# Combine weights of the routed rounds: spread to all partitions by a DMA instead of a one-hot matrix product and a copy from PSUM

## The chip, the cores and the metric

One core of a Trainium2 chip runs the whole program. The metric is the device time of one execution in microseconds (us), median of the runs shown. TensorE (PE) multiplies, VectorE (DVE), ScalarE (ACT) and GpSimd (POOL) work elementwise, SyncE (SP) issues DMAs. Each engine takes its own instructions in order, and they wait for one another on semaphores.

## The reference

The program is a chain of eight blocks on 4 x 256 tokens of 128 features: four attention blocks and four feed-forward blocks, each added to x. The change touches the second block only, four rounds of a mixture of four experts with two chosen for each token:

```python
def more_forward(x, Wg, bg, W1, b1, W2, b2):     # x: layer norm of the stream, 1024 tokens x 128
    cur = x
    for r in range(4):
        flat = cur.reshape(-1, h)
        logits = flat @ Wg[r] + bg[r]
        vals, idx = jax.lax.top_k(logits, 2)
        w = jax.nn.softmax(vals, axis=-1)
        cw = jnp.sum(jax.nn.one_hot(idx, 4) * w[..., None], axis=1)      # 1024 x 4, zero for the experts not chosen
        hmid = jax.nn.gelu(jnp.einsum('nh,ehf->enf', flat, W1) + b1[:, None, :])   # 512 hidden features
        y = jnp.einsum('enf,efh->enh', hmid, W2) + b2[:, None, :]
        cur = cur + jnp.einsum('ne,enh->nh', cw, y).reshape(b, s, h)
    return cur
```

All experts are computed for all tokens, and the combine weight cw of an expert scales its output for each token.

## The kernel before

`routed_rounds` (line 1270) computes this with features on the partitions and tokens along the free dimension. The 1024 tokens are two halves of 512. A **turn** s is one round of one half (8 turns, the halves in alternation), and an **item** g = 4s + e is one expert e in one turn (32 items). What an item does:

- TensorE, `up(g)` (L1349): 12 products of 128x128 by 128x512, four feature tiles times three passes of a high and low split of the operands. `down(g)` (L1359): 12 more, into one PSUM bank.
- ScalarE, `hidden(g)` (L1434): the gelu of the four tiles out of PSUM, and a copy of half of them as high part (L1439). GpSimd copies the other half (L1590).
- VectorE, `split_hidden(g)` (L1504): the low parts. `combine(g)` (L1539, L1541): (down + b2) times the combine weight, then added to the running tokens curT.

Once in a turn there is the routing: `route(s)` (L1370) for the logits, some 18 tiny VectorE operations (`choose_first`, `choose_second`, `weigh_two`, the last at L1524), a tanh on ScalarE (L1462), `turn_weights(s)` (L1377), which transposes the weights to 4 rows (experts) x 512 tokens in PSUM bank 6, and `take_weights(s)` (L1458), ScalarE's copy of these rows into the tile cwT (partitions 0 to 3).

`combine` needs the row of its expert on all 128 partitions, since features are on partitions and the weight belongs to the token. Before the change `split_weights(s)` (VectorE, L1529) adds a low part of the four rows at partitions 32 to 35. `spread_weights(g)` (TensorE, L1389) multiplies a one-hot matrix `choose` of 36x128 by cwT (36x512) into bank 7, which puts row e on all partitions, and `take_spread(g)` (ScalarE, L1445) copies bank 7 to the tile spread[e]. There are four spread tiles, one for each expert. Two zeroings on ScalarE and two GpSimd operations (L1582) build `choose` and the rows of zeros once, before the first turn.

The order is written out by hand. In loop step g TensorE issues up(g), then the turn's transposes if a turn begins (e is 0), spread_weights(g-1), the routing product of the next turn if e is 1, and down(g-1). VectorE issues the routing operations due in this step, split_hidden(g), split_weights(s) if a turn begins, and combine(g-1). ScalarE issues hidden(g), take_weights(s) if a turn begins, and take_spread(g-1). SyncE has nothing in this stage before the change. Its next DMAs (L652, four loads for the following block) stand right behind the block before.

Of the kernel before, what the change touches and what calls it, by code (L numbers as in the profile page):

```python
# [23 lines left out]
P = 128  # L24
# [1245 lines left out]
def routed_rounds(k, name, number, E, W, ahead):  # L1270
# [11 lines left out]
    TURNS = 2 * ROUNDS  # L1282
    ITEMS = TURNS * E
    TPH = NT // 2
    LOW = 32
    shape = [P, TPH, E]
    hidden_part = [[k.parts[i][:, b * FT * HALF:(b + 1) * FT * HALF].rearrange("p (f n) -> p f n", f=FT) for b in range(2)]
                   for i in range(2)]
    cur_part = [k.parts[i][:, 2 * FT * HALF:2 * FT * HALF + T] for i in range(2)]
    cwT, choose = k.parts[2][:, 0:T], k.parts[2][:, T:T + E * P]  # L1290
    rows_of_parts = (slice(0, E), slice(LOW, LOW + E))
    w1_part = [k.split[i][:, 0:E * HALF].rearrange("p (e f) -> p e f", e=E) for i in range(2)]
    w2_part = [k.split[i][:, E * HALF:2 * E * HALF].rearrange("p (e f d) -> p e f d", e=E, f=FT) for i in range(2)]
    k.carve_from(0)
    H = [k.carve(F32, FT, HALF) for _ in range(2)]
    spread = [k.carve(F32, HALF) for _ in range(E)]
    logits, tagged, sel1, sel2, low, cw = (k.carve(F32, TPH, E) for _ in range(6))
    m1, m2, top, th, w1, w2 = (k.carve(F32, TPH) for _ in range(6))
    weighted = k.xn[:, :, :].rearrange("p t d -> p (t d)")
# [8 lines left out]
    tanh_ready = count("tanh_ready", TURNS)  # L1308
    cw_ready = count("cw_ready", TURNS)
    cwT_psum = count("cwT_psum", TURNS)  # L1310
    cwT_high = count("cwT_sb", TURNS)
    cwT_low = count("b2_psum", TURNS)
    spread_psum = k.count("rounds_spread_psum", ITEMS)
    cur_high = count("turned", TURNS)
    cur_low = count("T_ready", TURNS)
    up_psum = count("up_psum", FT * ITEMS)
    h_ready = count("h_ready", FT * ITEMS)
    down_psum = count("down_psum", ITEMS)
    combined = count("combined", ITEMS)
    chooser = k.count("rounds_chooser", 2)  # L1320
    rows_psum = k.count("rounds_rows_psum", 2)
    spread_sb = k.count("rounds_spread_sb", ITEMS)
    zeros = k.count("rounds_zeros", 2)
    high_pool = k.count("rounds_h_high", ITEMS)
    k.slots_filled = k.count("packed_fill_done", 4)
    FILL_AT = 8
# [11 lines left out]
    def tensor(pe):  # L1338
        bank = k.bank

        def up(g):
            s, e = g // E, g % E
            if e == 0:
                pe.wait_ge(*cur_low.at(s + 1))
            for f in range(FT):
                if g >= 1:
                    pe.wait_ge(*h_ready.at(FT * (g - 1) + f + 1))
                for n, (a, b) in enumerate(PASSES):
                    ins = pe.matmul(bank[f], w1_part[a][:, e, f * P:(f + 1) * P], cur_part[b][:, half_of(s % 2)],  # L1349
                                    start=n == 0, stop=n == len(PASSES) - 1)  # L1350
                ins.then_inc(up_psum.semaphore, 1)

        def down(g):
            if g >= 2:
                pe.wait_ge(*combined.at(g - 1))
            for f in range(FT):
                pe.wait_ge(*h_low.at(2 * g + f // 2 + 1))
                for n, (a, b) in enumerate(PASSES):
                    ins = pe.matmul(bank[4 + g % 2], w2_part[a][:, g % E, f, :], hidden_part[b][g % 2][:, f, :],  # L1359
                                    start=f == 0 and n == 0, stop=f == FT - 1 and n == len(PASSES) - 1)  # L1360
            ins.then_inc(down_psum.semaphore, 1)

        def route(s):
            if s >= 2:
                pe.wait_ge(*combined.at(E * (s - 1)))
            if s >= 1:
                pe.wait_ge(*cwT_low.at(s))
            for t in range(TPH):
                at = (s % 2) * HALF + t * P
                ins = pe.matmul(bank[6][:, t * E:(t + 1) * E], curT[:, at:at + P], W("router")[:, s // 2, :],  # L1370
                                start=True, stop=True)
            ins.then_inc(logits_psum.semaphore, 1)

        def turn_weights(s):
            pe.wait_ge(*cw_ready.at(s + 1))
            for t in range(TPH):
                ins = pe.transpose(bank[6][0:E, t * P:(t + 1) * P], cw[:, t, :], k.ident[:, :])  # L1377
            ins.then_inc(cwT_psum.semaphore, 1)

        def spread_weights(g):  # L1380

            s, e = g // E, g % E
            if e == 0:
                pe.wait_ge(*cwT_low.at(s + 1))
                if s == 0:
                    pe.wait_ge(*chooser.at(2))
            if g >= 1:
                pe.wait_ge(*spread_sb.at(g))
            pe.matmul(bank[7], choose[0:LOW + E, e * P:(e + 1) * P], cwT[0:LOW + E, half_of(s % 2)],  # L1389
                      start=True, stop=True).then_inc(spread_psum.semaphore, 1)  # L1390

        def rows_of(h, dst):
            pe.wait_ge(*combined.at(ITEMS - E * (1 - h)))
            for t in range(TPH):
                at = h * HALF + t * P
                ins = pe.transpose(dst[:, t * P:(t + 1) * P], curT[:, at:at + P], k.ident[:, :])
            ins.then_inc(rows_psum.semaphore, 1)

        k.norm.tensor(pe, use, k.xn)
        pe.wait_ge(k.norm.T_ready, 2 * use + 2)  # L1400
        pe.wait_ge(k.weights[name], 16)
        route(0)
        pe.wait_ge(ahead.parts_ready, 1)
        for g in range(ITEMS + 1):
            s, e = g // E, g % E
            if g < ITEMS:
                up(g)
            if g == 1:
                turn_weights(0)
            elif e == 0 and 0 < s < TURNS:  # L1410
                turn_weights(s)
            if g > 1:
                spread_weights(g - 1)
            if e == 1 and 0 < s + 1 < TURNS:
                route(s + 1)
            if g >= 1:
                down(g - 1)
            if g == 1:
                spread_weights(0)
            if g == ITEMS - 1:  # L1420
                rows_of(0, bank[6])
        rows_of(1, bank[0])

    def scalar(act):
# [13 lines left out]
            act.wait_ge(*h_ready.at(FT * (g + 1)))  # L1438
            act.activation(two(hidden_part[0][g % 2], 1), two(H[g % 2], 1), ACT.Copy).then_inc(high_act.semaphore, 1)  # L1439

        def take_spread(g):
            act.wait_ge(*spread_psum.at(g + 1))
            if g >= E:
                act.wait_ge(*combined.at(g - E + 1))
            act.activation(spread[g % E], bank[7], ACT.Copy).then_inc(spread_sb.semaphore, 1)  # L1445

        def split_current(s):
            if s >= 2:
                act.wait_ge(*combined.at(E * (s - 1)))
# [3 lines left out]

        def take_weights(s):
            act.wait_ge(*cwT_psum.at(s + 1))
            if s == 0:
                act.wait_ge(*chooser.at(2))
            act.activation(cwT[0:E, half_of(s % 2)], bank[6][0:E, :], ACT.Copy).then_inc(cwT_high.semaphore, 1)  # L1458

        def weigh(s):  # L1460
            act.wait_ge(*margin.at(s + 1))
            act.activation(th, m2, ACT.Tanh, scale=0.5).then_inc(tanh_ready.semaphore, 1)  # L1462

        act.wait_ge(k.x_tiles, NT * number)
        for part, words in ((cwT[0:LOW, :], T), (choose[0:LOW + E, :], E * P)):
            n = part.shape[0]
            act.activation(part.rearrange("p (a n) -> p a n", n=P), k.ident[0:n, :].unsqueeze(1).broadcast_to([n, words // P, P]),
                           ACT.Copy, scale=0.0).then_inc(zeros.semaphore, 1)
        k.norm.scalar(act, use, curT)
        split_current(0)  # L1470
        split_current(1)
        for g in range(ITEMS + 1):
# [10 lines left out]
                take_weights(s)  # L1483
            if e == 1 and 2 <= s + 1 < TURNS:
                split_current(s + 1)
            if g >= 1:
                take_spread(g - 1)

    def vector(dve, chain):
        bank = k.bank  # L1490
# [32 lines left out]
            chain.then(dve.tensor_tensor(sel2, sel2, w2.unsqueeze(2).broadcast_to(shape), ALU.mult))  # L1523
            dve.tensor_tensor(cw, sel1, sel2, ALU.add).then_inc(cw_ready.semaphore, 1)  # L1524

        def split_weights(s):
            dve.wait_ge(*cwT_high.at(s + 1))
            cols = half_of(s % 2)
            dve.tensor_tensor(cwT[LOW:LOW + E, cols], bank[6][0:E, :], cwT[0:E, cols].bitcast(F32), ALU.subtract)\  # L1529
                .then_inc(cwT_low.semaphore, 1)  # L1530

        def combine(g):
            s, e = g // E, g % E
            dve.wait_ge(*down_psum.at(g + 1))
            dve.wait_ge(*spread_sb.at(g + 1))
            if g >= 2:
                dve.wait_ge(*combined.at(g))
            mine, cols = weighted[:, half_of(g % 2)], half_of(s % 2)
# [14 lines left out]
        for g in range(ITEMS + 1):  # L1553
# [10 lines left out]
                choose_second(s + 1)  # L1564
            if g < ITEMS:
                split_hidden(g)
            if g == 1:
                split_weights(0)
            elif e == 0 and 0 < s < TURNS:
                split_weights(s)  # L1570
            if g >= 1:
                combine(g - 1)
        add_rows(0, bank[6])
# [2 lines left out]

    def gpsimd(pool):
        k.norm.gpsimd(pool, use)
        pool.wait_ge(*zeros.at(2))
        for part in rows_of_parts:  # L1580
            rows = choose[part, :].rearrange("p (e n) -> p e n", e=E)
            pool.affine_select(out=rows, in_=rows.bitcast(F32), compare_op=ALU.not_equal, fill=1.0, base=0,  # L1582
                               pattern=[[-1, E], [0, P]], channel_multiplier=1).then_inc(chooser.semaphore, 1)
            n = rows_of_parts.index(part) + 1
            pool.wait_ge(*chooser.at(n))
        for g in range(ITEMS):
            if g >= 2:
                pool.wait_ge(*down_psum.at(g - 1))
# [5 lines left out]
                    .then_inc(k.slots_filled.semaphore, 1)  # L1594

    def sync(sp):
        pass

    return tensor, scalar, vector, gpsimd, sync

# [1443 lines left out]
class Kit:  # L3044
# [92 lines left out]
    def open_rounds(self):  # L3137

        self.work_extent.close()
        self.work_extent.enter_context(self.nc.sbuf_tensor("kept_for_l1x", [P, REGION_B], F32))  # L3140
        parts = 2 * PARTS + T + HALF
        flat = self.work_extent.enter_context(self.nc.sbuf_tensor("parts", [P, parts], F32R))
        self.parts = [flat[:, 0:PARTS], flat[:, PARTS:2 * PARTS], flat[:, 2 * PARTS:]]
        self.work = self.work_extent.enter_context(self.nc.sbuf_tensor("rounds_work", [P, WORK - REGION_B - parts], F32))

    def open_later(self):
# [266 lines left out]
```

## Time and profile before

| | us |
|---|---|
| runs | 1202.22, 1204.62, 1211.36 |
| median | 1204.62 |
| span of the profiled execution | 1202.7 |

| engine | busy us | share of the span |
|---|---|---|
| TensorE | 1047.4 | 87% |
| VectorE | 811.3 | 67% |
| ScalarE | 665.8 | 55% |
| GpSimd | 387.2 | 32% |

These shares are means over eight blocks. The routed rounds are the stretch from about 124 to 347 us of the span. Busy times of an engine are sums of its instructions. "issue" as the releaser of a wait means that the engine waited for nothing that the profile shows. PEld is TensorE's load of the stationary operand, which can run beside a product. In a view of DMAs the stretch asked for is cut into 40 equal slices, and each value is the rate of one slice in GB/s, or the mean busy share of the core's 16 DMA engines in tenths.

### The profile page before, as it was taken

To read this page: it belongs to the slowest core of one execution; us is meant where nothing else is said; L and a number is where in the kernel's file an instruction comes from. 1 tells how busy PE (TensorE), PEld (TensorE's weight loads), DVE (VectorE), ACT (ScalarE), POOL (GpSimd) and SP (SyncE) were. 2 spreads that over 40 slices of the span, in tenths; PEclk is the share of its full clock that TensorE was granted. 3 is DMA by queue.
4 is the path that set the end of the run, shared out by engine and by line. 5 is a ranking of instruction groups with operands and counts; after the bars stand their busy time and mean duration, and the time that the engine had idled before them with its cause. 6 is when DMAs were issued, how large, how long until landed. Compare 5 with 4: busy or idle time off the path is not lost.

```text
span 1202.7 us, 18102 instructions
## 1 busy us (share of the span) xinstructions
PE 1047.4 (87%) x5942; PEld 735.0 (61%) x5942; DVE 811.3 (67%) x1977; ACT 665.8 (55%) x1640; POOL 387.2 (32%) x608
## 2 busy tenths in 40 slices
PE   3587899999976989878899999998699899999677
PEld 2345677777741333655667677776568566668565
DVE  5763588887866867258788777667755566665563
ACT  3253566666642757456677877777134466665121
POOL 5220112111111101034655657557300344443200
PEclk8687799999985989989899999999599999999779
DMA  6503000000004330030000000030600100000000
GB/s 217 111 10 104 1 1 6 9 1 1 1 26 145 132 91 3 1 140 1 1 1 1 1 1 1 1 140 1 251 1 2 72 2 1 2 1 2 1 1 18
DMA packets 26572, 45.08 MB, mean 37 GB/s; under 512 B 3536, under 2 KB 23792, under 8 KB 25200
## 3 DMA queue, kind: packets, MB, share of 16 engines
q1 hardware_dynamic: 23936, 41.57, 10.2%
q10 hardware_dynamic: 2544, 2.36, 0.6%
q8 instruction: 48, 0.79, 0.3%
q14 instruction: 44, 0.36, 0.1%
HBM read 36.94 MB, written 6.82 MB: 36 GB/s over the span
## 4 chain that ended last, share of the span: by engine, by line
PE 41%; ACT 9%; DVE 8%; issue 3%; POOL 2%; DMA 1%; DVEq 0%; SPq 0%; ACTq 0%; POOLq 0%
PE psum L1736 7%; ACT region_d L1802 4%; PE psum L2397 3%; PE psum L2450 3%; PE psum L2381 2%; ACT region_c L1819 2%; PE psum L2364 2%; PE psum L1773 2%; PE psum L1750 2%; PE psum L2359 2%; PE psum L2807 1%; PE psum L409 1%; PE psum L2356 1%; PE psum L2404 1%; PE psum L1053 1%
## 5 line engine op out<-in xcount | busy, mean ns | idle before, releaser
L1736 PE MATMUL psum<-gated_parts 128*128 128x512 f32 x768 | 198.8, 412 | 15.0 <-DVE region_d L1906 10.9
L1736 PEld LDWEIGHTS psum<-gated_parts 128*128 128x128 f32 x768 | 141.3, 192 | 68.3 <-DVE region_d L1906 30.9
L1987 POOL TENSOR_TENSOR region_d<-region_d 128x256 f32<-128x256 f32 x126 | 99.5, 790 | 114.4 <-DVE region_d L1906 114.0
L1434 ACT ACTIVATE rounds_work<-psum,region_c 128x512 f32<-128x512 f32 x128 | 87.0, 689 | 59.3 <-PE psum L1349 59.3
L787 DVE TENSOR_REDUCE work<-psum 128x1 f32<-128x512 f32 x128 | 81.8, 685 | 28.0 <-PE psum L365 26.4
L1359 PE MATMUL psum<-parts,split 128*128 128x512 f32 x384 | 97.6, 404 | 0.0
L1802 ACT ACTIVATE region_d<-psum,gated_work 128x128 f32<-128x128 f32 x256 | 75.8, 451 | 36.8 <-issue 26.2
L1349 PE MATMUL psum<-parts,split 128*128 128x512 f32 x384 | 94.4, 396 | 0.0
L1590 POOL CAST parts<-rounds_work 128x1024 fp32r<-128x1024 f32 x32 | 33.4, 1044 | 179.7 <-ACT rounds_work L1434 179.7
L1504 DVE TENSOR_TENSOR parts<-rounds_work,parts 128x1024 fp32r<-128x1024 f32 x64 | 77.5, 1223 | 20.3 <-POOL parts L1590 17.4
L1906 DVE SCALAR_TENSOR_TENSOR region_d<-psum,gated_work,region_d 128x128 f32<-128x128 f32 x256 | 71.4, 344 | 29.0 <-ACT region_d L1802 20.6
L1906 DVE SCALAR_TENSOR_TENSOR region_d<-psum,ctx,region_d 128x128 f32<-128x128 f32 x256 | 71.4, 343 | 24.1 <-ACT region_d L1802 21.0
L2475 ACT ACTIVATE null_work<-psum,null_work 128x257 f32<-128x257 f32 x128 | 59.7, 472 | 47.9 <-DVE null_work L2533 47.9
L1802 ACT ACTIVATE region_d<-psum,ctx 128x128 f32<-128x128 f32 x256 | 73.5, 383 | 20.5 <-PE psum L1736 16.3
L1349 PEld LDWEIGHTS psum<-parts,split 128*128 128x128 f32 x384 | 73.5, 192 | 15.7 <-issue 0.2
L1359 PEld LDWEIGHTS psum<-parts,split 128*128 128x128 f32 x384 | 70.9, 191 | 19.6 <-issue 6.1
L545 ACT ACTIVATE work<-psum 128x1024 f32<-128x1024 f32 x64 | 65.1, 1024 | 26.6 <-PE psum L379 24.2
L133 POOL TENSOR_TENSOR rstd<-var_eps,minus_half 128x4 f32<-128x4 f32 x12 | 12.3, 1023 | 186.8 <-DVE var_eps L93 186.7
L2533 DVE TENSOR_REDUCE null_work<-psum 128x2 f32<-128x514 f32 x64 | 43.9, 688 | 38.4 <-PE psum L2381 38.4
L2621 POOL TENSOR_TENSOR null_work<-null_work 128x512 f32<-128x512 f32 x64 | 66.6, 1040 | 0.0
L365 PE MATMUL psum<-work 48*128 48x512 bf16 x128 | 53.0, 450 | 13.7 <-DMA work<-q_parts 10.5
L2546 DVE COPY null_work<-psum 128x512 f32<-128x512 f32 x64 | 43.3, 678 | 4.0 <-PE psum L2397 3.6
(433 smaller groups left out, 2189.4 us busy)
## 6 DMA issues: line engine op xcount, KB each, us to landing
region_a<-in_l1v SPq DMA_DIRECT2D x1, 4096.0 KB, 14.4
region_b_last<-in_l1o SPq DMA_DIRECT2D x1, 4096.0 KB, 12.4
region_a<-in_l2f SPq DMA_DIRECT2D x1, 4096.0 KB, 13.5
region_b_last<-in_l3f_small SPq DMA_DIRECT2D x1, 4096.0 KB, 19.8
region_a<-in_l3f SPq DMA_DIRECT2D x1, 2080.0 KB, 7.3
region_c<-in_l0f SPq DMA_DIRECT2D x1, 2076.0 KB, 12.2
region_c<-in_l3x SPq DMA_DIRECT2D x1, 2048.0 KB, 7.9
ctx_parts<-front_work SPq DMA_DIRECT2D x6, 256.0 KB, 3.8
```

Of the source, the lines that this page charges most:

```text
L545: act.activation(PT[s % 2].rearrange("p (a n) -> p a n", a=2), k.pair(2 + 2 * (s % 2)), ACT.Exp, scale=scale).then_inc(p2_exp.semaphore, 1)
L787: dve.tensor_reduce(NM[:, b, heads[0]:heads[0] + HPG, t], bank[g % 2][:, :].rearrange("p (j n) -> p j n", j=HPG), AX.X, ALU.max, negate=Tr ...
L1349: ins = pe.matmul(bank[f], w1_part[a][:, e, f * P:(f + 1) * P], cur_part[b][:, half_of(s % 2)], start=n == 0, stop=n == len(PASSES) - 1)
L1359: ins = pe.matmul(bank[4 + g % 2], w2_part[a][:, g % E, f, :], hidden_part[b][g % 2][:, f, :], start=f == 0 and n == 0, stop=f == FT - 1 a ...
L1434: act.activation(H[g % 2][:, f, :], bank[f], ACT.Gelu_apprx_tanh, bias=W("b1")[:, (g % E) * FT + f:(g % E) * FT + f + 1]).then_inc(h_ready ...
L1504: dve.tensor_tensor(two(hidden_part[1][g % 2], c), two(H[g % 2], c), two(hidden_part[0][g % 2], c).bitcast(F32), ALU.subtract).then_inc(h_ ...
L1736: ins = pe.matmul(bank[2 * (n % 2) + c], src[a][:, t * P:(t + 1) * P], weights[b][:, piece(c)], start=m == 0, stop=m == len(PASSES) - 1)
L1802: ins = act.activation(scaled[n % RING][:, e, :], bank[2 * (n % 2)][:, e * P:(e + 1) * P], ACT.Copy, scale=scalars[:, n % NT, e:e + 1])
L1906: ins = dve.scalar_tensor_tensor(out=tile, in0=bank[2 * (n % 2) + 1][:, e * P:(e + 1) * P], scalar=scalars[:, n % NT, HALF_E + e:HALF_E + ...
L1987: pool.tensor_tensor(tile[:, 0:2, :], tile[:, 0:2, :], tile[:, 2:4, :], ALU.add).then_inc(k.pool_chain, 1)
L2475: ins = act.activation(PR[g % 4][:, t, :], bank[2 * (g % 2) + t][:, 0:NK], ACT.Exp, bias=NM[:, g % 4, t:t + 1], accum_out=den[:, g % 4, t: ...
L2621: pool.tensor_tensor(PR[g % 4][:, :, 0:S], PR[g % 4][:, :, 0:S], r.broadcast_to([P, TPB, S]), ALU.mult)\
```

## The change

For each turn, SyncE waits until the four rows are in cwT and issues one DMA for each expert, which reads that expert's row of 512 fp32 values (2 KB, one partition) 128 times and writes spread[e] on all 128 partitions (256 KB). From the second turn on, each DMA also waits until the last turn's combine of the same expert has read spread[e]. The one-hot product, its ScalarE copy, the low part of the rows, the one-hot matrix and its set-up go. cwT is now plain fp32.

```diff
-        def spread_weights(g):
-            s, e = g // E, g % E
-            if e == 0:
-                pe.wait_ge(*cwT_low.at(s + 1))
...
-            pe.matmul(bank[7], choose[0:LOW + E, e * P:(e + 1) * P], cwT[0:LOW + E, half_of(s % 2)],
-                      start=True, stop=True).then_inc(spread_psum.semaphore, 1)
...
-        def take_spread(g):
-            act.wait_ge(*spread_psum.at(g + 1))
-            if g >= E:
-                act.wait_ge(*combined.at(g - E + 1))
-            act.activation(spread[g % E], bank[7], ACT.Copy).then_inc(spread_sb.semaphore, 1)
...
-        def split_weights(s):
-            dve.wait_ge(*cwT_high.at(s + 1))
-            cols = half_of(s % 2)
-            dve.tensor_tensor(cwT[LOW:LOW + E, cols], bank[6][0:E, :], cwT[0:E, cols].bitcast(F32), ALU.subtract)\
-                .then_inc(cwT_low.semaphore, 1)
...
             if s >= 1:
-                pe.wait_ge(*cwT_low.at(s))
+                pe.wait_ge(*cwT_sb.at(s))
...
             dve.wait_ge(*down_psum.at(g + 1))
-            dve.wait_ge(*spread_sb.at(g + 1))
+            dve.wait_ge(*spread_loaded[e].at(16 * (s + 1)))
...
     def sync(sp):
-        pass
+        for s in range(TURNS):
+            sp.wait_ge(*cwT_sb.at(s + 1))
+            for e in range(E):
+                if s >= 1:
+                    sp.wait_ge(*combined.at(E * (s - 1) + e + 1))
+                sp.dma_start(spread[e], cwT[e:e + 1, half_of(s % 2)].unsqueeze(1).broadcast_to([1, P, HALF])).then_inc(spread_loaded[e].semaphore, 16)
```

SyncE, between the weight loads that end the first block (in_l2f_small) and the loads for the third (ctx_parts), the change against before:

```order
+L1549 DMA rounds_work<-rounds_work 128x1x512 [waits experts_cwT_sb]
+L1549 DMA rounds_work<-rounds_work 128x1x512 x3
+L1549 DMA rounds_work<-rounds_work 128x1x512 [waits experts_combined,experts_cwT_sb]
+L1549 DMA rounds_work<-rounds_work 128x1x512 [waits experts_combined] x3
 L652 DMA work<-ctx_parts 48x4x256 [waits c_stored,packed_fill_done]
 L652 DMA work<-ctx_parts 48x4x256
```

The pair of rows of the second turn comes seven times, for turns 1 to 7: 32 DMAs stand ahead of the four loads L652, which were next in line before.

TensorE at the start of turn 2, before (L1377 are the transposes, L1389 the one-hot product, L1359 down, L1349 up):

```order
L1377 MATMUL psum<-ident,rounds_work 4x128 [waits experts_cw_ready]
L1377 MATMUL psum<-ident,rounds_work 4x128 x3
L1389 MATMUL psum<-parts 128x512 [waits rounds_spread_sb]
L1359 MATMUL psum<-parts,split 128x512 [waits rounds_h_low,experts_combined]
L1359 MATMUL psum<-parts,split 128x512 x2
```

and with the change (L1371 are the transposes, L1353 is down):

```order
L1371 MATMUL psum<-ident,rounds_work 4x128 [waits experts_cw_ready]
L1371 MATMUL psum<-ident,rounds_work 4x128 x3
L1353 MATMUL psum<-parts,split 128x512 [waits rounds_h_low,experts_combined]
L1353 MATMUL psum<-parts,split 128x512 x2
L1353 MATMUL psum<-parts,split 128x512 [waits rounds_h_low]
```

The one-hot product is gone from between up and down, and nothing takes its place on this engine.

VectorE at the start of a turn, before:

```order
L1504 TENSOR_TENSOR parts<-rounds_work,parts 128x1024 [waits rounds_h_high]
L1504 TENSOR_TENSOR parts<-rounds_work,parts 128x1024 [waits rounds_high_act]
L1529 TENSOR_TENSOR parts<-psum,parts 4x512 [waits experts_cwT_sb]
L1539 SCALAR_TENSOR_TENSOR xn<-psum,region_c,rounds_work 128x512 [waits experts_combined,rounds_spread_sb,experts_down_psum]
L1541 TENSOR_TENSOR xnT<-xnT,xn 128x512 [waits vector_chain]
```

and with the change (L1467 are the low parts of the hidden tiles, L1496 and L1498 the combine of the last item of the turn before):

```order
L1467 TENSOR_TENSOR parts<-rounds_work,parts 128x1024 [waits rounds_h_high]
L1467 TENSOR_TENSOR parts<-rounds_work,parts 128x1024 [waits rounds_high_act]
L1496 SCALAR_TENSOR_TENSOR xn<-psum,region_c,rounds_work 128x512 [waits experts_combined,rounds_spread3,experts_down_psum]
L1498 TENSOR_TENSOR xnT<-xnT,xn 128x512 [waits vector_chain]
L1467 TENSOR_TENSOR parts<-rounds_work,parts 128x1024 [waits rounds_h_high]
L1467 TENSOR_TENSOR parts<-rounds_work,parts 128x1024 [waits rounds_high_act]
```

The split of the weights is gone, and each combine waits for the DMA of its expert (`rounds_spread3`), with the low parts of the next item queued behind it.

## Rows read from the trace of the kernel before

**Rows 1.** The page's first line: the profiled execution.
```profile
span 1202.7 us, 18102 instructions
```

**Rows 2.** Busy time by stretch: routed rounds, then one turn of them.
```profile
core 0: us, PE busy (x) PEld busy (x) DVE busy (x) ACT busy (x) POOL busy (x), PEclk, DMA share, GB/s
140.00:345.00 205.00, 200.65 (x857) 151.81 (x857) 159.33 (x261) 136.50 (x202) 34.92 (x34) 0.99 0.01 3
188.50:214.55 26.05, 25.43 (x113) 19.41 (x112) 21.07 (x37) 17.76 (x28) 6.84 (x7) 1.00 0.06 16
```

**Rows 3.** Who waited for whom, 140 to 345 us: total, times, longest us.
```profile
PEld psum L1389 <- issue: 10.2, 32, 0.4
PE psum L1377 <- DVE rounds_work L1524: 4.4, 7, 0.6
```

**Rows 4.** Timeline of TensorE across items: start us, us, engine, line, xcount [idle before].
```profile
204.45 2.88 PE L1349 MATMUL psum<-parts,split 128*128 128x512 f32 x12
207.26 0.50 PE L1389 MATMUL psum<-parts 36*128 36x512 f32 x1
207.69 2.99 PE L1359 MATMUL psum<-parts,split 128*128 128x512 f32 x12
210.52 2.88 PE L1349 MATMUL psum<-parts,split 128*128 128x512 f32 x12
```

**Rows 5.** Timeline, all engines, where a turn begins.
```profile
210.72 0.75 DVE L1539 SCALAR_TENSOR_TENSOR xn<-psum,region_c,rounds_work 128x512 f32<-128x512 f32 x1 [0.24 <-PE psum L1359]
211.50 0.69 DVE L1541 TENSOR_TENSOR xnT<-xnT,xn 128x512 f32<-128x512 f32 x1
...
212.93 1.03 DVE L1524 TENSOR_TENSOR rounds_work<-rounds_work 128x16 f32<-128x16 f32 x1
...
214.02 0.60 PE L1377 MATMUL psum<-ident,rounds_work 128*4 128x128 f32 x4 [0.62 <-DVE rounds_work L1524]
...
215.18 0.57 ACT L1458 ACTIVATE parts<-psum 4x512 fp32r<-4x512 f32 x1
...
216.56 0.68 DVE L1529 TENSOR_TENSOR parts<-psum,parts 4x512 fp32r<-4x512 f32 x1
```

**Rows 6.** Timeline where the first turn's weights are ready.
```profile
136.29 0.59 ACT L1458 ACTIVATE parts<-psum 4x512 fp32r<-4x512 f32 x1 [0.20 <-PE psum L1377]
137.90 0.68 DVE L1529 TENSOR_TENSOR parts<-psum,parts 4x512 fp32r<-4x512 f32 x1
...
140.36 4.62 PE L1359 MATMUL psum<-parts,split 128*128 128x512 f32 x12
```

**Rows 7.** Timeline at the stage's end: the last combine.
```profile
346.57 0.69 DVE L1541 TENSOR_TENSOR xnT<-xnT,xn 128x512 f32<-128x512 f32 x1
```

**Rows 8.** DMA issues of the page: mask_bias; then two stretches' GB/s, 15.8:16.4 and 17.6:18.2.
```profile
front_work<-mask_bias SPq DMA_DIRECT2D x4, 4.0 KB
...
GB/s 0 0 0 0 0 0 0 0 0 0 0 0 0 0 0 0 0 0 0 0 0 0 0 0 0 0 0 0 0 68 0 69 0 34 34 0 35 34 0 0
...
GB/s 0 0 0 0 0 0 0 0 0 0 0 0 0 0 0 0 0 0 0 0 0 0 0 34 34 68 1 34 1 34 34 0 34 0 0 0 0 0 0 0
```

**Rows 9.** DMA share and GB/s, 38:42; then one window, 100 to 101 us.
```profile
DMA  9999999989999999999999999999999999999999
GB/s 251 246 256 215 200 190 200 184 149 215 220 246 287 266 174 159 179 189 149 118 118 159 133 118 118 133 154 169 179 174 169 154 154 226 236 241 195 215 277 246
...
front_work<-q_parts SPq DMA_DIRECT2D x3, 64.0 KB
...
100.00:101.00 1.00, 1.00 (x9) 0.75 (x11) 0.00 (x0) 0.98 (x1) 0.00 (x0) 0.50 1.02 428
```

**Rows 10.** SyncE's timeline in the stage; then GB/s by slice, 208:214.
```profile
208.79 1.79 SPq L652 DMA_DIRECT2D work<-ctx_parts  x4
...
GB/s 0 0 0 0 0 0 0 0 0 0 0 34 150 208 191 188 171 219 205 171 212 181 150 137 242 157 7 0 0 0 0 0 0 0 0 0 0 0 0 0
```

More of the change, by code:

```diff
@@ L1284, in routed_rounds @@
     TPH = NT // 2
-    LOW = 32
     shape = [P, TPH, E]
@@ L1289, in routed_rounds @@
     cur_part = [k.parts[i][:, 2 * FT * HALF:2 * FT * HALF + T] for i in range(2)]
-    cwT, choose = k.parts[2][:, 0:T], k.parts[2][:, T:T + E * P]
-    rows_of_parts = (slice(0, E), slice(LOW, LOW + E))
     w1_part = [k.split[i][:, 0:E * HALF].rearrange("p (e f) -> p e f", e=E) for i in range(2)]
@@ L1296, in routed_rounds @@
     spread = [k.carve(F32, HALF) for _ in range(E)]
+    cwT = k.carve(F32, T)
     logits, tagged, sel1, sel2, low, cw = (k.carve(F32, TPH, E) for _ in range(6))
@@ L1310, in routed_rounds @@
     cwT_psum = count("cwT_psum", TURNS)
-    cwT_high = count("cwT_sb", TURNS)
-    cwT_low = count("b2_psum", TURNS)
-    spread_psum = k.count("rounds_spread_psum", ITEMS)
+    cwT_sb = count("cwT_sb", TURNS)
+    spread_loaded = [k.count(f"rounds_spread{e}", 16 * TURNS) for e in range(E)]
     cur_high = count("turned", TURNS)
@@ L1411, in tensor @@
                 turn_weights(s)
-            if g > 1:
-                spread_weights(g - 1)
             if e == 1 and 0 < s + 1 < TURNS:
@@ L1417, in tensor @@
                 down(g - 1)
-            if g == 1:
-                spread_weights(0)
             if g == ITEMS - 1:
@@ L1455, in take_weights @@
             act.wait_ge(*cwT_psum.at(s + 1))
-            if s == 0:
-                act.wait_ge(*chooser.at(2))
-            act.activation(cwT[0:E, half_of(s % 2)], bank[6][0:E, :], ACT.Copy).then_inc(cwT_high.semaphore, 1)
+            act.activation(cwT[0:E, half_of(s % 2)], bank[6][0:E, :], ACT.Copy).then_inc(cwT_sb.semaphore, 1)
         def weigh(s):
@@ L1462, in weigh @@
             act.activation(th, m2, ACT.Tanh, scale=0.5).then_inc(tanh_ready.semaphore, 1)
[L1464 to L1468, printed above, removed]
         k.norm.scalar(act, use, curT)
@@ L1485, in scalar @@
                 split_current(s + 1)
-            if g >= 1:
-                take_spread(g - 1)
     def vector(dve, chain):
@@ L1566, in vector @@
                 split_hidden(g)
[L1567 to L1570, printed above, removed]
             if g >= 1:
@@ L1578, in gpsimd @@
         k.norm.gpsimd(pool, use)
[L1579 to L1585, printed above, removed]
         for g in range(ITEMS):
@@ L3140, in open_rounds @@
         self.work_extent.enter_context(self.nc.sbuf_tensor("kept_for_l1x", [P, REGION_B], F32))
-        parts = 2 * PARTS + T + HALF
+        parts = 2 * PARTS
         flat = self.work_extent.enter_context(self.nc.sbuf_tensor("parts", [P, parts], F32R))
-        self.parts = [flat[:, 0:PARTS], flat[:, PARTS:2 * PARTS], flat[:, 2 * PARTS:]]
+        self.parts = [flat[:, 0:PARTS], flat[:, PARTS:2 * PARTS]]
         self.work = self.work_extent.enter_context(self.nc.sbuf_tensor("rounds_work", [P, WORK - REGION_B - parts], F32))
```

7 lines of the change are left out of this document (removed).

## The prediction

> **What bounds the kernel now.** I read the busy times by stretch first. In the routed rounds TensorE is busy 200.65 of 205 us at a granted clock of 0.99, VectorE 159.33, and the DMA engines 0.01 of the time [rows 2]. So TensorE sets this stage, and the DMA side is free. A turn of four items is 26.05 us, with VectorE busy 21.07 of it, so VectorE is the next bound, five us behind. The waits say the same: TensorE's idle time in the stage is some 0.32 us ahead of each of the 32 one-hot products (10.2 us in all, "issue") and 4.4 us ahead of the transposes L1377, for VectorE [rows 3]. The timeline gives the item: up starts at 204.45 and the next up at 210.52, which is 6.07 us, 0.43 of it from the one-hot product to down (207.26 to 207.69) [rows 4].
>
> **What the change takes away.** On TensorE, 32 products of 0.43 us, and up to 0.32 us of idle time ahead of each: 13.8 to 24 us of the engine that sets the stage. On ScalarE (17.76 us busy in a turn) and VectorE it takes a copy in each item and L1529 in each turn (0.68 us [rows 5]). ScalarE is hidden behind TensorE today, so that is worth nothing by itself. The first routing product after the start no longer waits for L1529 but for ScalarE's copy, 138.58 against 136.88 [rows 6], which is 1.7 us. The set-up of the one-hot matrix stood beside the layer norm and is costed at nothing. What hides it is TensorE's wait for the norm, and it is gone in any case.
>
> **What the change adds.** 32 DMAs of 256 KB. Each reads one row of one partition 128 times. Combine(g) waits for its DMA. Behind combine(g-1) on VectorE stand the routing operations of the next step and the low parts of item g+1. TensorE's down(g+1) waits for these, and so, in the end, does everything.
>
> What one such DMA costs is the question. 256 KB over all partitions would be short: the load between 100 and 101 us moved 428 GB/s with the 16 engines full [rows 9], so 0.6 us plus latency. The trace has two kinds of transfer that don't reach this. The loads of 38 to 42 us, 64 KB ones among them, go to few partitions (16 to 48). There the engines are as busy (share 9 tenths and more in nearly every slice), but the rate falls to 118 GB/s [rows 9]. Full engines and a quarter of the rate mean that the packets wait for something on the side of the few partitions. The nearest relative of the new DMA is mask_bias: 4 KB in 8 packets of 512 B, all from a row on one partition, as here [rows 8]. Each slice is 15 ns, so 34 GB/s in a slice is one packet. The first packets start in the 30th slice and the last in the 38th, 120 ns for seven steps. In the other stretch it is the 24th to the 33rd slice, 135 ns. That is 17.1 and 19.3 ns for 512 B, 26 to 30 GB/s, though eight packets could be on eight engines at once. For 2 KB it is 69 to 77 ns, and for 128 of them 8.8 to 9.9 us. With an uncertainty of a slice each way (105 to 150 ns) it is 7.7 to 11.0 us. I take 9.6 us, between the mean of the two stretches (9.3) and the slower of them, since the first packets find the source idle and these seven steps are short for a steady rate.
>
> The Trainium skill has a rule for this (SBUF — State Buffer, "Door 1: The DMA port swizzle"): DMA bandwidth goes with the number of ports that the partitions reach, 27.2 GB/s each, and partitions 0 to 3 share one port. Rows 8 and the fall in rows 9 agree with it. By it the four rows of cwT have one port together, a DMA is 262144 B / 27.2 GB/s = 9.64 us as an estimate, and the stage would come out 1.3 us later than by my price.
>
> **Does the stream stay full?** If the transfers of one turn follow one another, a turn of DMAs is 4 x 9.6 = 38.4 us against TensorE's 26.05. At a turn's start there could be a gap, because the next rows wait for routing. From the start of a combine (210.72) to the end of ScalarE's copy of the rows (215.75) it is 5.03 us [rows 5]. From issue to the first bytes it is 0.86 us (208.79 to the 12th slice of 0.15 us, 209.65 [rows 10]). Together 5.9 us. This chain starts when the third DMA of a turn has landed, and the fourth then runs for another 9.6 us. So the next turn's first DMA is in the queue 3.7 us before the fourth ends: no gap. The wait for the old spread tile is behind by a whole turn for experts 0 to 2, and for expert 3 it ends 1.5 us after the fourth landed, when three others are queued.
>
> TensorE will now wait, and its clock may fall. At the lower level of its clock 12 products took 4.62 us [rows 6], so an item takes 9.24 us. That is still under 9.6, and routing adds a little. So even then the DMAs set the pace. The price of a low clock is 0 to 5 us in all, and I take 0. The loads L652 go from 208.79 us to behind all 32. They have 384 KB in all and took some 2.4 us [rows 10]. They land right behind the last spread, before the next block has made its own operands, so they cost nothing. If that cover is missing, it is those 2.4 us.
>
> **The sum.** The first rows are ready at 136.88 [rows 6]. First bytes 0.86 later: 137.7. 32 x 9.6 = 307.2, so the last byte at 444.9. About 1 us until the wait ends (no row shows it, 0 to 2), and 1.5 us for combine (0.75 + 0.69 with gaps, rows 5): 447.4. Before, the last combine ends at 347.26 [rows 7]. The stage ends 100.1 us later, the rest is unchanged, and TensorE's 14 to 24 us are lost behind the wait. 1202.7 [rows 1] + 100.1 = 1302.8. The median of the runs is 1.9 above this execution: **1304.7**, so 1305 us. With 7.7 and 11.0 us for a DMA it is 1244 and 1350.
>
> **Rivals.** (A) The above, slower by 100 us: 82%.
>
> (B) Reading one row many times is no limit, and a DMA lands within some 3 us of its issue. For it: in rows 8 the engines' queues may just have been fed at this pace. The skill's fit (DMA: Bandwidth & Descriptors, "Anatomy of one DMA"; about 2.0 us plus bytes at 436 GB/s, measured for GpSimd's queue) would give 2.6 us as an estimate. Against it: two kinds of transfer, the fewer partitions the slower. Then the DMA is hidden: the rows are ready at 215.75, and the turn's first combine comes an item and a half later. TensorE gives back 0.43 + 0.32 us in 32 items, 24 us, and 1.7 at the start. VectorE's chain ahead of L1377 doesn't get shorter, so that wait grows by up to 0.75 us in seven turns, 5 us back. 1204.6 - 21 = about 1184. The point from which it decides is a price below 5.3 us an item (6.07 - 0.75), 50 GB/s from one partition. 12%.
>
> (C) Something between: 5.5 to 7 us. Equality is where 32 items take as long as now: (347.26 - 2.5 - 137.7) / 32 = 6.5 us. Turns would then show gaps of 5.9 us less the price. 1185 to 1220, 3%.
>
> (D) Many engines on one row hinder each other more than in rows 8, over 11 us: above 1350, 3%. The floor, 118 GB/s over 16 partitions, would give 7.4 GB/s and 35 us, but rows 8 exclude this.
>
> (E) The DMA doesn't use 16 engines but few or one. That changes little in time if one engine moves about 27 GB/s (428 / 16 in rows 9), 9.8 us for 256 KB. It is a variant of A by its time, within its chance, and told apart by the DMA share: near one sixteenth here, near full in A.
>
> **How the numbers follow.** A is the likeliest and gives the time. 1265 to 1350 us is 8.4 to 11.0 us for a DMA and holds nearly all of A, about 8 in 10. About 1% is what a measurement of this kernel tells from no change. Slower by over 1%: A, D and a bit of C, 0.85. Faster: B and a bit of C, 0.13. Within 1%: the rest of C, 0.02.
>
> **What would show it.** The rounds last from 124 to about 447 us. SyncE's issues come in groups by turns of 38 us. DMA moves some 27 GB/s throughout, with the 16 engines' share near full. VectorE's largest wait is combine for its DMA, and TensorE waits for VectorE's low parts, with a busy share near 60% in the stage. Wrong would be: DMAs that land 3 us after issue (B), a share near 0.06 (E), gaps in the DMA rate at each turn's start (the 3.7 us margin wrong), or a price above 11 us (D).

## The result, and the profile after

The change makes the kernel slower: 1311.24 us, the median of 4 runs (1302.69 to 1315.7), against 1206.09 us before (4 runs, 1202.22 to 1211.36). The ratio is 1.0866, with a 95% interval of 1.0831 to 1.0902. The profiled execution has a span of 1307.3 us, 104.6 more than before [rows 1].

The page of the kernel after, first line, and its 40 slices of the span. The spreads take slices 5 to 14:

```profile
span 1307.3 us, 17993 instructions
...
PEclk8686977788878667899898999999969989999979
DMA  5421688888888652300200000003050010000000
GB/s 211 91 58 46 22 27 28 28 28 27 28 28 27 30 157 68 137 2 17 113 1 1 2 1 1 1 1 129 1 232 1 26 42 1 1 2 1 1 1 17
```

The rate stands at 27 to 28 GB/s for 300 us, while the 16 DMA engines are busy 8 tenths of the time and more. This is a flat ceiling, and not a series of short transfers with gaps. Before, the whole stage moved 3 GB/s [rows 2]. Busy time by stretch says the same for the rounds:

```profile
core 0: us, PE busy (x) PEld busy (x) DVE busy (x) ACT busy (x) POOL busy (x), PEclk, DMA share, GB/s
140.00:447.00 307.00, 208.69 (x820) 164.99 (x819) 143.64 (x254) 119.56 (x170) 40.65 (x34) 0.81 0.88 28
```

TensorE went from 200.65 of 205 us busy at a clock of 0.99 [rows 2] to 208.69 of 307 at 0.81. Its busy time did not fall, although it has 32 products less: part of it runs at the lower level of its clock. The timeline of the first spreads and the last, and the line of SyncE's DMA in the view of one source line:

```profile
137.00 17.19 SPq L1549 DMA_DIRECT2D rounds_work<-rounds_work  x4
...
148.95 0.75 DVE L1496 SCALAR_TENSOR_TENSOR xn<-psum,region_c,rounds_work 128x512 f32<-128x512 f32 x1 [10.99 <-DMA rounds_work<-rounds_work]
...
159.55 0.75 DVE L1496 SCALAR_TENSOR_TENSOR xn<-psum,region_c,rounds_work 128x512 f32<-128x512 f32 x1 [5.18 <-DMA rounds_work<-rounds_work]
...
447.31 0.75 DVE L1496 SCALAR_TENSOR_TENSOR xn<-psum,region_c,rounds_work 128x512 f32<-128x512 f32 x1 [5.14 <-DMA rounds_work<-rounds_work]
448.10 0.69 DVE L1498 TENSOR_TENSOR xnT<-xnT,xn 128x512 f32<-128x512 f32 x1
...
DMA to landing us min/median/max: 11.9/27.2/34.1
```

From the first combine (148.95) to the last (447.31) are 31 spreads: 9.62 us each, 27.2 GB/s. The first spread has nothing ahead of it in the queue and lands in 11.9 us, so some 2.3 us of it is latency. The later ones are issued while others are under way, up to 34.1 us ahead of their landing. Who waited for whom, from 124 to 455 us (us in total, times, longest):

```profile
DVE xn L1496 <- issue: 119.5, 24, 6.1
...
PE psum L1371 <- DVE rounds_work L1487: 74.2, 8, 11.6
...
DVE xn L1496 <- DMA rounds_work<-rounds_work: 21.3, 3, 11.0
```

"issue" hides a DMA here. The combine waits 24 times with no releaser named, and these waits are 5.0 us on average, like two of the three that the profile puts down to the DMA (5.18 and 5.14; the third, of 11.0, is the first spread). The reader should check such a line against the landings before believing it.

### The profile page after: what moved, and what is told of

Same layout as the page of the kernel before. It is cut to its first block, busy times and chain, and to the rows that moved or that the text cites. A ratio compares the mean times of both kernels' runs of the same rounds, so it can differ in the third digit from the quotient of the medians.

```text
span 1307.3 us, 17993 instructions
## 1 busy us (share of the span) xinstructions
PE 1062.9 (81%) x5910; PEld 751.4 (57%) x5910; DVE 794.9 (61%) x1969; ACT 646.3 (49%) x1606; POOL 391.1 (30%) x606
## 4 chain that ended last, share of the span: by engine, by line
PE 38%; ACT 8%; DVE 8%; issue 3%; POOL 1%; DMA 0%; DVEq 0%; SPq 0%; ACTq 0%; POOLq 0%
PE psum L1688 6%; ACT region_d L1754 4%; PE psum L2349 3%; PE psum L2402 2%; PE psum L2333 2%; ACT region_c L1771 2%; PE psum L2316 2%; PE psum L1725 2%; PE psum L1702 2%; PE psum L2311 2%; PE psum L2759 1%; PE psum L409 1%; PE psum L2308 1%; PE psum L2356 1%; PE psum L1053 1%
## 5 line engine op out<-in xcount | busy, mean ns | idle before, releaser
L1688 PE MATMUL psum<-gated_parts 128*128 128x512 f32 x768 | 198.7, 411 | 14.9 <-DVE region_d L1858 10.7
L1353 PE MATMUL psum<-parts,split 128*128 128x512 f32 x384 | 119.2, 471 | 8.7 <-DVE parts L1467 8.7
L1496 DVE SCALAR_TENSOR_TENSOR xn<-psum,region_c,rounds_work 128x512 f32<-128x512 f32 x32 | 24.0, 751 | 160.6 <-issue 119.5
L1536 POOL CAST parts<-rounds_work 128x1024 fp32r<-128x1024 f32 x32 | 39.1, 1223 | 259.4 <-ACT rounds_work L1412 259.4
L1353 PEld LDWEIGHTS psum<-parts,split 128*128 128x128 f32 x384 | 88.8, 236 | 30.3 <-issue 9.7
L1343 PE MATMUL psum<-parts,split 128*128 128x512 f32 x384 | 96.0, 401 | 0.0
L1343 PEld LDWEIGHTS psum<-parts,split 128*128 128x128 f32 x384 | 75.2, 196 | 16.6
L1467 DVE TENSOR_TENSOR parts<-rounds_work,parts 128x1024 fp32r<-128x1024 f32 x64 | 76.2, 1231 | 2.7 <-ACT parts L1417 1.3
L1371 PE MATMUL psum<-ident,rounds_work 128*4 128x128 f32 x32 | 7.7, 392 | 74.2 <-DVE rounds_work L1487 74.2
## 6 DMA issues: line engine op xcount, KB each, us to landing
rounds_work<-rounds_work SPq DMA_DIRECT2D x32, 256.0 KB, 27.2
```

What stands on the lines that cost most here:

```text
L1467: dve.tensor_tensor(two(hidden_part[1][g % 2], c), two(H[g % 2], c), two(hidden_part[0][g % 2], c).bitcast(F32), ALU.subtract).then_inc(h_ ...
L1688: ins = pe.matmul(bank[2 * (n % 2) + c], src[a][:, t * P:(t + 1) * P], weights[b][:, piece(c)], start=m == 0, stop=m == len(PASSES) - 1)
```

## The experiments

### Where the rows are read from

**e1: the rows through HBM.** SyncE stores the turn's four rows (8 KB) and the spreads read them there, still 128 reads of one row.

```diff
             sp.wait_ge(*cwT_sb.at(s + 1))
+            sp.dma_start(k.rows_dram[E * s:E * s + E, :], cwT[0:E, half_of(s % 2)]).then_inc(spread_loaded[0].semaphore, 16)
+            sp.wait_ge(*spread_loaded[0].at(32 * s + 16))
             for e in range(E):
...
-                sp.dma_start(spread[e], cwT[e:e + 1, half_of(s % 2)].unsqueeze(1).broadcast_to([1, P, HALF]))...
+                sp.dma_start(spread[e], k.rows_dram[E * s + e:E * s + e + 1, :].rearrange("a n -> (a n)").partition_broadcast(P))...
```

> For each turn the four rows (8 KB) are first stored to HBM, and the four spreads then read them there, each still 128 reads of one 2 KB row and 128 writes to the same partitions of spread[e]. Theory (reading one SBUF partition gives some 27 GB/s, and 9.6 us for a spread): the limit is gone, a spread lands some 5 to 6 us after the rows are ready and is hidden, TensorE sets the stage again and has 0.43 + 0.32 us less in each item: 1180 to 1195 us, DMA share in the stage about 0.1. Rival (128 rows of 2 KB written in one DMA are slow whatever the source, or issue and waits on SyncE's queue are what costs): 1300 us or more.

Measured: 1195.05 us, ratio 0.9915 (0.9881 to 0.995). So it is not the 128 writes, nor the queue. It is also 0.9% faster than the kernel before, at the upper end of what was expected. The issues of DMAs in 140 to 330 us, with the median time to landing, and SyncE's timeline at one turn:

```profile
rounds_work<-cw_rows SPq DMA_DIRECT2D x28, 256.0 KB, 3.7
...
208.13 0.27 SPq L1546 DMA_DIRECT2D cw_rows<-rounds_work  x1
209.53 2.60 SPq L1551 DMA_DIRECT2D rounds_work<-cw_rows  x4
```

The same 256 KB land in 3.7 us in place of 27.2, or of 11.9 for the spread that had nothing ahead of it. The way over HBM costs 1.4 us (208.13 to 209.53), which lies beside TensorE's down and up.

**e2: from SBUF, but from 128 partitions.** The source is `W("w1")[:, e, :]`, a resident weight tile, in place of the row. The combine weights are left out by this.

> The spreads of the changed kernel, but each reads 128 different partitions of a resident weight tile (same bytes, same 2 KB rows, same queue and waits) in place of one row 128 times. The combine weights are left out of the result by this. Theory (one source partition): lands within 3 us of issue, TensorE sets the stage, 1180 to 1195 us. Rival (copies from SBUF to SBUF, or DMAs of this size on this queue, are slow as such): 9.6 us each as before, 1305 us.

Measured: 1193.62 us, ratio 0.9907 (0.9857 to 0.9957). The view of its DMA line:

```profile
DMA to landing us min/median/max: 2.2/2.4/4.1
```

From SBUF to SBUF, the same bytes on the same queue need 2.4 us. What was slow is the one partition, or its port.

**e4 and e5: two sources, on different ports or on the same.** ScalarE copies the rows a second time, to partitions AT2 to AT2 + 3, and issues the spreads of experts 1 and 3 from there on its own queue. e4 has AT2 = 64, e5 has AT2 = 32. Nothing else differs.

```diff
+            act.activation(cwT[AT2:AT2 + E, half_of(s % 2)], bank[6][0:E, :], ACT.Copy).then_inc(cwT_two.semaphore, 1)
             act.activation(cwT[0:E, half_of(s % 2)], bank[6][0:E, :], ACT.Copy).then_inc(cwT_sb.semaphore, 1)
+            spread_odd(s, 1)
+        def spread_odd(s, e):
...
+            act.dma_start(spread[e], cwT[AT2 + e:AT2 + e + 1, half_of(s % 2)].unsqueeze(1).broadcast_to([1, P, HALF]))...
...
+            if (g == 2 or e == 1 and s > 0) and s < TURNS:
+                spread_odd(s, 3)
...
-            for e in range(E):
+            for e in (0, 2):
```

> ScalarE copies the four rows of a turn twice, to partitions 0 to 3 and to 64 to 67. Experts 0 and 2 are spread from the first copy by SyncE's queue, experts 1 and 3 from the second by ScalarE's queue. Theory (the limit is the source side's port, and partitions 64 to 67 lie on another port): two streams of 27 GB/s side by side, 2 x 9.6 = 19.3 us of each in a turn, under TensorE's 23, so 1185 to 1205 us with the extra work of ScalarE. Rival 1 (a limit of the whole DMA side for such broadcasts): 1300 us or more. Rival 2 (a limit of the partition or its row): as theory here, told apart by the run with the second copy at partition 32.

> The same kernel with the second copy at partitions 32 to 35, which by the port theory share the port of partitions 0 to 3. Theory (port): the two streams share 27 GB/s, 38.5 us a turn, 1300 to 1320 us. Rival 2 (limit of one partition or of one row read many times): two partitions, so two streams, 1185 to 1205 us as with the second copy at 64.

Measured: e4 1284.53 us (1.0661, 1.0608 to 1.0714), e5 1345.85 us (1.117, 1.1112 to 1.1228). As times both miss. The rates decide all the same. The 40 slices of 140 to 330 us, e4 first:

```profile
GB/s 28 41 26 35 50 40 0 12 27 46 55 48 29 8 0 22 27 40 31 44 59 2 8 27 43 35 52 44 15 0 16 27 47 56 47 27 5 0 27 31
```

and e5:

```profile
GB/s 27 27 28 31 27 28 27 17 9 27 27 28 28 26 31 27 25 0 27 27 27 28 29 28 28 27 9 19 28 27 27 27 28 28 26 12 13 28 28 27
```

With the second copy at partition 64 the rate reaches 50 to 59 GB/s in five slices. With the second copy at 32 it stays at 27 to 28, though two queues read two different partitions. The slices at 31 hold some other small transfer. So the limit isn't the row or the partition, and not the DMA side as a whole. It is something that partitions 0 to 3 share with 32 to 35 but not with 64 to 67. The Trainium skill names it (SBUF — State Buffer, "Door 1: The DMA port swizzle"): bit 5 of the partition's number keeps the port, bit 6 changes it, and a port gives 27.2 GB/s. The trace agrees to the digit with 27.2 for one.

Why e4's time isn't 1190 the trace shows in part. Its rate falls to 0 to 8 GB/s five times in the view above, about once in a turn, so its turns are a chain and not a stream. ScalarE issues the spread of expert 1 at 175.29 us and SyncE that of expert 0 at 175.90. From 176 to 184 us only ScalarE's queue (q10) moves packets, at one port's rate. Both queues move in the second stretch, 187 to 195 us:

```profile
DMA packets 107, 0.22 MB, mean 27 GB/s; under 512 B 0, under 2 KB 0, under 8 KB 107
q10 hardware_dynamic: 107, 0.22, 85.3%
...
DMA packets 227, 0.43 MB, mean 54 GB/s; under 512 B 17, under 2 KB 17, under 8 KB 227
q1 hardware_dynamic: 111, 0.20, 51.0%
q10 hardware_dynamic: 116, 0.23, 44.7%
...
195.92 0.75 DVE L1508 SCALAR_TENSOR_TENSOR xn<-psum,region_c,rounds_work 128x512 f32<-128x512 f32 x1 [13.28 <-DMA rounds_work<-rounds_work]
```

So expert 0's spread, which the first combine of the turn needs, starts when expert 1's is nearly through, and it lands 20 us after its issue. The next rows are ready some 16 us after that combine (211.65). The stretches from 212 to 220 and 248 to 256 us look the same. VectorE waits 101.5 us for these DMAs in seven waits. The late issue of expert 3 (180.44), behind ScalarE's hidden(4s+1), is not the cause here: expert 1's packets are still under way then. Why the second queue's packets start so late stays open, and I didn't try other orders. e5 has the same gaps at one port's rate, which makes it 34.6 us slower than the change itself.

**e3: three quarters of the bytes.** The spread is cut to 384 columns, and the tiles are filled with 0.25 once. The weights of the last 128 tokens of each half are left out by this.

```diff
-                sp.dma_start(spread[e], cwT[e:e + 1, half_of(s % 2)].unsqueeze(1).broadcast_to([1, P, HALF]))...
+                sp.dma_start(spread[e][:, 0:384], cwT[e:e + 1, (s % 2) * HALF:(s % 2) * HALF + 384].unsqueeze(1).broadcast_to([1, P, 384]))...
```

> The changed kernel with each spread cut to 384 of its 512 tokens, 192 KB in place of 256, still 128 reads from one partition, and the tiles filled with 0.25 once. The weights of a quarter of the tokens are left out by this. Theory (a fixed rate of 27.5 GB/s from one port, no gap between turns since 7.15 us is over the 5.9 us of the routing chain): 32 x 7.15 = 229 us in place of 305 to 308, the rounds end at some 371 us, and the whole is 1231 us (1222 to 1242). Rival (a price for each packet or for each DMA, not for bytes): 1290 us or more. Rival (gaps at the turns' start appear): above 1245 us.

Measured: 1234.91 us, ratio 1.0237 (1.0171 to 1.0304). The last combine, and the rate in 40 slices from 150 to 360 us:

```profile
373.40 0.69 DVE L1499 TENSOR_TENSOR xnT<-xnT,xn 128x512 f32<-128x512 f32 x1
...
GB/s 30 28 27 27 27 28 28 30 27 30 27 28 28 28 31 27 28 27 27 28 30 27 27 28 27 32 27 28 27 28 29 28 27 30 28 28 27 28 27 27
```

The rounds end at 374.09, 74.7 us before those of the change, although the first spread is issued 2.4 us later (139.4 against 137.0), behind the filling of the tiles. From the first issue it is 77.1 us less for 32 x 64 KB less, 27.2 GB/s: the price goes with bytes. Smaller packets (1.5 KB) have the same rate.

### What the one-hot product had cost

e1 gains 8.4 us and e2 9.8 us on the kernel before, where the prediction's rival B has 21. The next runs ask why, and how much of it needs a DMA at all.

**e6: the kernel before, one-hot product 128 rows deep.** The rows added are zero.

```diff
-            pe.matmul(bank[7], choose[0:LOW + E, e * P:(e + 1) * P], cwT[0:LOW + E, half_of(s % 2)],
+            pe.matmul(bank[7], choose[:, e * P:(e + 1) * P], cwT[:, half_of(s % 2)],
...
-        for part, words in ((cwT[0:LOW, :], T), (choose[0:LOW + E, :], E * P)):
+        for part, words in ((cwT[:, :], T), (choose[:, :], E * P)):
```

> The kernel before, with the one-hot product made 128 rows deep in place of 36 (the rows added are zero), so that all of TensorE's products in the loop but the transposes have 128x128 operands. Theory (part of an item's price for this product is the change of shape: 0.3 us of idle ahead of it and a load that isn't covered): an item falls from 6.07 us to some 5.7, the rounds end 8 to 12 us earlier, and some of it is lost to a longer wait at the transposes and to the clock in the next block: 1190 to 1200 us. Rival (the price is the product's own, or the wait instruction's): item 6.07, 1202 to 1206 us.

Measured: 1194.44 us, ratio 0.9903 (0.9874 to 0.9932), from 10 runs. TensorE's timeline, for comparison with [rows 4]:

```profile
202.91 2.88 PE L1349 MATMUL psum<-parts,split 128*128 128x512 f32 x12
205.63 0.39 PE L1389 MATMUL psum<-parts 128*128 128x512 f32 x1
205.86 2.88 PE L1359 MATMUL psum<-parts,split 128*128 128x512 f32 x12
208.58 2.88 PE L1349 MATMUL psum<-parts,split 128*128 128x512 f32 x12
...
212.52 0.60 PE L1377 MATMUL psum<-ident,rounds_work 128*4 128x128 f32 x4 [1.06 <-DVE rounds_work L1524]
```

The slot of the product is 0.23 us (205.63 to 205.86) in place of 0.43, the idle time ahead of it is gone, and the item is 5.67 us in place of 6.07. More rows of zeros cost less than fewer rows. The rounds end at 339.41, 7.9 us earlier than before, just under the 8 to 12 expected. With no DMA at all this run is as fast as e1 (1195.05). The Trainium skill has the likely reason (TensorEngine Tiling (Array Packing), "Key Properties"): a change of tiling mode drains TensorE. The run shows the 0.4 us, not the mode.

**e7: the kernel through HBM, transposes moved.** TensorE's wait ahead of the transposes had grown, from 6.5 us in eight waits before the change. The view of waits of e1, 124 to 331 us:

```profile
PE psum L1371 <- DVE rounds_work L1487: 12.8, 8, 2.3
```

In e7 they are issued behind down(g-1), when VectorE is done:

```diff
-            elif e == 0 and 0 < s < TURNS:
-                turn_weights(s)
             if e == 1 and 0 < s + 1 < TURNS:
                 route(s + 1)
             if g >= 1:
                 down(g - 1)
+            if e == 0 and 0 < s < TURNS:
+                turn_weights(s)
```

> The kernel with the rows through HBM, and TensorE's transposes of the weights (L1371) moved behind down(g-1) instead of between up and down at the start of a turn. In the run before they cost TensorE 12.8 us of waiting for VectorE (4.4 before the change). Theory: that wait goes, the rows come some 2.7 us later and the spread is still nearly hidden, so the rounds end 5 to 12 us earlier than at 330.5 us and the whole is at 1180 to 1192 us. Rival (VectorE, busy 163 of 205 us with its gaps, is the bound by now, and TensorE only waits elsewhere): the rounds end within 2 us of 330.5, 1193 to 1197 us.

Measured: 1182.24 us, ratio 0.9773 (0.9708 to 0.9838). A repeat beside e8 (label e9) gave 1181.18 us, 0.9784 (0.9741 to 0.9827). TensorE's timeline at a turn's start:

```profile
201.70 2.88 PE L1343 MATMUL psum<-parts,split 128*128 128x512 f32 x12
204.42 2.88 PE L1353 MATMUL psum<-parts,split 128*128 128x512 f32 x12
207.14 0.60 PE L1371 MATMUL psum<-ident,rounds_work 128*4 128x128 f32 x4
207.50 3.00 PE L1343 MATMUL psum<-parts,split 128*128 128x512 f32 x12
```

No wait is left there. The item is 5.44 us (2 x 2.72), and the rounds end at 321.51 us against 330.46 in e1 and 347.26 before [rows 7].

**e8: the kernel before with both repairs,** the one-hot product 128 rows deep and the transposes behind down(g-1). **e9** is e7 again, on the same chip.

> The kernel before with both repairs: the one-hot product 128 rows deep, and TensorE's transposes of the weights behind down(g-1). No DMA. Theory (what the spread by DMA still gives after both is one product slot of 0.22 us in each item on TensorE, 7 us in all, less what VectorE's extra operations cost nothing): the rounds end 6 to 9 us after the 321.5 us of the kernel through HBM with the transposes moved, 326 to 331 us, and the whole is 1183 to 1192 us. Rival (VectorE or ScalarE, with their extra copies, are the bound by now): rounds end above 333 us, 1192 us or more.

> The kernel through HBM with the transposes moved, unchanged, on the same chip as the repaired one-hot kernel: 1178 to 1186 us, 5 to 10 us under it if the DMA still gives something, equal if not.

Measured: e8 1190.85 us, ratio 0.9884 (0.9823 to 0.9944); e9 0.9784. The rounds of e8 end at 331.53, half a us later than expected, those of e9 at 320.96. So a spread by DMA, from a source that isn't one port, ends the rounds 10.6 us earlier, and some 9.6 of that are its own. It saves 32 slots of 0.23 us (7.4), 1.7 us where the first routing product waits for L1529 (2.4 us against 0.7), and 0.6 us of set-up: from the first transpose of the layer norm to the first routing product it is 3.79 us in e8 (121.14 to 124.93) and 3.18 in e9 (120.09 to 123.27). The remaining 1 us lies ahead of the rounds, where e8's execution is 1.05 us later for no reason of the spread's. The whole differs by 9.7 us.

**Where the rest of the gain went.** e1's rounds end 16.8 us earlier than before, but the whole is 8.9 us shorter in the profiled executions (1202.7 and 1193.8). Between the issue of the load in_l1v and that of in_l1o, the second part of the next block, which the change doesn't touch, before and e1:

```profile
411.70:512.10 100.40, 89.99 (x862) 45.82 (x861) 56.71 (x92) 60.35 (x78) 8.26 (x24) 0.93 0.18 61
```

```profile
396.50:504.70 108.20, 99.23 (x862) 48.68 (x861) 56.84 (x92) 60.86 (x78) 8.25 (x24) 0.83 0.16 57
```

The same 862 matrix products take 99.23 us in place of 89.99, at a granted clock of 0.83 in place of 0.93, and the stretch is 7.8 us longer. That stretch lasts 104.9 us in e3, 105.1 in e2, 110.9 in e7 and 104.8 in its repeat e9. In the kernel before, the change, e4, e5, e6 and e8 it is 100.3 to 101.4. e7 and e9 are the same kernel and differ by 6 us here. So the clock of that block varies, from one execution to another too, and costs 4 to 10 us. There is one profile for each kernel, and whether the rounds' end has a part in it isn't shown.

## Why the prediction was right, point by point

- **The price of a spread, 9.6 us.** Measured 9.62. The taken value came from two stretches of 0.6 us with eight packets each [rows 8]. The relative was right, one source partition read many times, and e5 against e4 shows that the reason is the port of the source. Rows 8 could not tell that: those copies also write to one partition (line 692 of the kernel), so source and destination were not told apart. The slices allowed 7.7 to 11.0 us, so that 9.6 came within 0.02 is luck. The 27.2 GB/s of the Trainium skill (9.64 us), named in the prediction, was equally near.
- **The stream stays full.** Right in time and cause: the rate doesn't fall between turns, and 31 spreads follow at 9.62 us. The rows of turns 1 to 7 are ready 5.2 to 6.5 us before the combine that takes the turn's fourth spread (turn 2: 211.15 against 216.39), where the prediction had 4.6 (9.6 less 5.03).
- **Start and end.** First rows at 136.97 (136.38 + 0.59) against 136.88 taken. The rounds end at 448.79 against 447.4, of which 0.8 us is 31 x 0.02 and 0.4 us the latency of the first spread (2.3 us in place of 0.86 + 1).
- **The rest unchanged.** This step missed by 3.1 us: from the last combine to the end of the span are 858.5 us in place of 855.4 (1202.7 - 347.26). The next block's first stretch, up to the issue of in_l1v, is longer: 69.1 us after the rounds' end in place of 64.4, and 1.6 of the 4.7 us come back later. So the span is 1307.3 where the sum has 1302.8. The median is 3.9 us above this execution in place of 1.9, and so 1311.2 where the sum has 1304.7.
- **The clock's price, 0 to 5 us, taken as 0.** In the rounds, where the clock fell to 0.81, it cost nothing that shows, since the DMAs set the pace. Behind them it did cost: the 4.7 us of the point above are the clock's. From the rounds' end to the issue of in_l1v, before and with the change:

```profile
347.26:411.70 64.44, 46.10 (x271) 16.23 (x271) 46.43 (x92) 24.53 (x34) 11.14 (x22) 0.71 0.30 90
448.79:517.93 69.14, 51.45 (x271) 17.85 (x271) 46.51 (x92) 24.43 (x34) 11.11 (x22) 0.63 0.28 84
```

  The same 271 products take 5.35 us more at a granted clock of 0.63 in place of 0.71.
- **An item at the lower clock, "still under 9.6".** This reading was wrong, and it did no harm by luck. The 4.62 us for 12 products [rows 6] stand in a stretch with a mean granted clock of 0.63 (140.36 to 145), so part of them ran at full speed. With the change one group of 12 products has a granted clock of 0.52 (259.1 to 264.5):

```profile
259.11 5.37 PE L1353 MATMUL psum<-parts,split 128*128 128x512 f32 x12
```

  That makes an item some 10.7 us as an estimate, above the 9.62 of a spread. A clock that stayed low would have set the pace instead of the DMAs. It didn't stay low: behind each long wait of the transposes the next product group is slow (4.33 us at 210.17, behind a wait of 10.24), and the one after it (2.90 us) is back at full speed.
- **Where TensorE waits.** Half right. I named down(g+1), for VectorE's low parts. In fact 74.2 us are waits of the transposes L1371 at a turn's start, and 8.7 us waits of down. VectorE's weights of the next turn stand behind the combine that waits for its DMA, and TensorE meets this once in a turn for some 9 us. TensorE's busy share is 68%, not near 60.
- **The engines' share near full, and rival E.** 0.88 with 28 GB/s, which is more than 14 of the 16 engines busy at the rate of one port. E is out.
- **Rival B's time.** It would have been 1184 us, and e1 and e2 show what that world gives: 1195.05 and 1193.62. Its term for the longer wait at the transposes was a little small (from 140 us on, 10.8 us in e1 against 4.4 [rows 3], so 6.4 in place of 5), and an item falls by 0.63 us (6.07 to 5.44), not by 0.75. The 0.32 us in it were misread: rows 3 give them to PEld, the weight loads, while the products themselves were idle for only 4.35 of 205 us [rows 2]. With 32 x 0.63 + 1.7 - 6.4 the rounds gain 15.5 us by its own sum. The set-up of the one-hot matrix, costed at nothing, is 0.6 us more (the 3.79 and 3.18 us of e8 and e9 also hold for the kernel before and the change). e1 has 16.8. In e1's execution the clock in the next block took nearly half of it, and rival B had no term for that.

## What to carry to other kernels

A DMA that spreads one row to all partitions is limited by its source: one SBUF port gives 27 GB/s, at partitions 0 to 3 as well as with 32 to 35 beside them, on one queue or two, and with all 16 engines taking part, so 256 KB cost 9.6 us, and four rows side by side on partitions 0 to 3 cost four times that. Store such rows to HBM first (1.4 us) and the spread lands in 3.7 us. When an engine is freed, look at once for the wait that was next: about half of the gain of the best kernel here (9.6 of 18.5 us in the profiled executions) came only when the transposes were moved behind the product that covers their wait. And repair what the old way costs before replacing it: zero rows and moved transposes, with no DMA, give 14.8 of the 24.4 us that e9 gains over the kernel before.

## What the runs showed of the hardware that was not expected

- A product 36 rows deep among others of 128 costs 0.4 us more than the same product filled up with zero rows to 128 (e6: item 5.67 us against 6.07). That alone is worth 1% of the kernel.
- 128 reads of one 2 KB row of HBM show no limit of that kind: 3.7 us to landing for 256 KB, against 2.4 us from 128 partitions of SBUF.
- Partitions 0 and 32 share a source port, and 0 and 64 don't: 27 to 28 GB/s against up to 59 in all.
- Spreads issued on two queues 0.6 us apart, from two ports, don't run side by side from the start: for 8 us only one queue moves packets, at 27 GB/s (e4, 176 to 184 us).
- The granted clock of a block that no edit touched varies: the same 862 products at 0.93 or 0.83, 90.0 or 99.2 us. What decides it is open.
